# Decoder layer on one core: GpSimd's context columns ahead of two reciprocals, one context unit between the turns of the normalised rows, and the second probabilities parted before the third exponentials

## The reference, cut to what matters

```python
x = x + _L0_attn_ref(_layernorm(x), W_A, W_V, W_O, b_O)
x = x + _L0_xattn_ref(_layernorm(x), ctx_1024, ctx_1024, WK, WV, WQ)
x = x + _L0_ffn_ref(_layernorm(x), router_w, wg_r, wu_r, wd_r, wg_s, wu_s, wd_s)
```

## Time and profile before

| what | value |
|---|---|
| median of 3 runs | 569.32 us (568.86 to 569.55) |
| the profiled execution, its own time | 569.86 us |
| span of its instructions | 568.1 us |
| TensorE busy | 542.3 us, 95% of the span |
| VectorE, ScalarE, GpSimd busy | 424.9, 257.4 and 201.2 us |
| mean granted TensorE clock | 0.996 of full speed |

### The profile page before, as it was taken

How to read it: one execution, slowest core, us unless ns; L and a number is a source line. 1 busy time by engine, 2 the same in 40 slices (tenths; PEclk the granted TensorE clock), 3 DMA queues, 4 the chain that set the end, 5 groups by cost and what they waited for, 6 DMA issues and landing times. The chain is left out here.

```text
span 568.1 us, 12928 instructions
## 1 busy us (share of the span) xinstructions
PE 542.3 (95%) x4716; PEld 369.6 (65%) x4716; DVE 424.9 (75%) x1101; ACT 257.4 (45%) x521; POOL 201.2 (35%) x246
## 2 busy tenths in 40 slices
PE   5799889999999999999999999999999998999997
PEld 4576557566776668666776668666866685666455
DVE  5867878778776697778886888678876876777654
ACT  4566657435354445435353545435543334332332
POOL 4225752214522154314512343334421343133123
PEclk9999989999999999999999999999999999999999
DMA  7988696793459823693459643994189216200341
GB/s 241 305 282 304 198 388 201 165 348 117 113 123 269 281 67 84 139 303 121 112 121 270 204 111 78 213 304 111 48 175 324 69 60 132 58 1 1 91 98 38
DMA packets 90734, 94.70 MB, mean 167 GB/s; under 512 B 28224, under 2 KB 76224, under 8 KB 90432
## 3 DMA queue, kind: packets, MB, share of 16 engines
q1 hardware_dynamic: 90688, 94.09, 58.7%
HBM read 75.66 MB, written 12.12 MB: 155 GB/s over the span
## 5 line engine op out<-in xcount | busy, mean ns | idle before, releaser
L700 POOL TENSOR_TENSOR mid<-gated,mid 128x512 f16<-128x512 f32 x72 | 86.4, 1200 | 214.2 <-ACT mid L909 214.1
L909 ACT ACTIVATE mid<-gated 128x512 f16<-128x512 f32 x72 | 45.0, 625 | 83.4 <-DVEq L1268 80.1
L142 PE MATMUL wide<-w_d,mid 128*128 128x256 f16 x288 | 78.5, 273 | 0.0
L144 PE MATMUL wide<-w_d,mid 128*128 128x256 f16 x288 | 78.5, 273 | 0.0
L143 PE MATMUL wide<-w_d,mid 128*128 128x256 f16 x288 | 78.5, 272 | 0.0
L1246 DVE SCALAR_TENSOR_TENSOR gated<-gated,score 128x512 f32<-128x512 f32 x72 | 49.2, 683 | 37.7 <-ACT gated L904 37.4
L142 PE MATMUL rows<-h3T,w_gu 128*128 128x512 f16 x160 | 60.7, 379 | 0.3 <-DVEq L122 0.3
L142 PE MATMUL score<-h3T,w_gu 128*128 128x512 f16 x160 | 60.7, 379 | 0.2
L143 PE MATMUL rows<-h3T,w_gu 128*128 128x512 f16 x160 | 60.6, 379 | 0.0
L144 PE MATMUL rows<-h3T,w_gu 128*128 128x512 f16 x160 | 60.6, 379 | 0.0
L144 PE MATMUL score<-h3T,w_gu 128*128 128x512 f16 x160 | 60.6, 379 | 0.0
(11 more groups left out here) (251 smaller groups left out, 1423.5 us busy)
## 6 DMA issues: line engine op xcount, KB each, us to landing
toep<-z_scratch SPq DMA_DIRECT2D x14, 2048.0 KB, 18.0
stage<-comb_scratch SPq DMA_DIRECT2D x32, 512.0 KB, 8.4
toep<-z_scratch SPq DMA_DIRECT2D x4, 1024.0 KB, 10.3
x_bo<-in_x SPq DMA_DIRECT2D x8, 512.0 KB, 11.7
x_in<-in_xr SPq DMA_DIRECT2D x7, 512.0 KB, 11.1
qT<-q_scratch SPq DMA_DIRECT2D x7, 512.0 KB, 3.8
vx<-v_scratch SPq DMA_DIRECT2D x7, 512.0 KB, 5.1
out<-x_out SPq DMA_DIRECT2D x7, 512.0 KB, 3.3
```

Source lines behind the costliest of these rows:

```text
L142: pe.matmul(out, stationary[0], moving[0], start=start, stop=False, **kw)
L144: return pe.matmul(out, stationary[1], moving[0], start=False, stop=stop, **kw)
L700: pool.tensor_tensor(mid_slot(j, 1, late), gate_slot(j, late), mid_slot(j, 0, late), ALU.subtract).then_inc(mid_split.sem, 1)
L909: act.activation(mid_slot(j, 0, late), gate_slot(j, late), ACT.Copy).then_inc(mid_hi.sem, 1)
```

## The change

Five edits, all in iterations 0 and 1; no instruction is added or taken away.

1. GpSimd, iteration 0: the columns of context 1 stand ahead of the reciprocal deviation of sequence 1's first norm. ScalarE's part of these columns stands ahead of the units of context 0 rather than between them.
2. GpSimd, iteration 1: the columns of context 5 stand ahead of the last reciprocal deviation (second half of the third norm).
3. Iteration 1, ScalarE and VectorE: unit 2 of context 3 and the second probabilities (`part_prob(.., 1)`) stand ahead of the third exponentials (ScalarE) and their sums (VectorE); VectorE's statistics of the next rows stand later.
4. TensorE, iteration 1: unit 0 of context 5 stands between the two halves of the turn of `h3`.
5. ScalarE and VectorE: unit 0 of context 5 stands ahead of the parting of `h3T`, unit 1 behind it.

```diff
@@ gpsimd, second_iteration
                 reciprocal_deviation(it - 1, 2)
+                part_context_columns(5)
                 reciprocal_deviation(it - 1, 2, 1)
-                part_context_columns(5)
@@ gpsimd, iteration
                 for j in range(MID):
...
-                    if f and not m and j == 2:
+                    if f and not m and j == 0:
                         part_context_columns(1)
                     if n and j == (4 if d else 1):
                         reciprocal_deviation(it + 1, 0)
@@ scalar, second_iteration
                 part_prob(it, it - 1, 0)
-                exp_scores(it, it - 1, 2)
-                part_context_columns(4)
                 act.wait_ge(w_lo, GATES_2 + 1)
                 part_context(3, (2,))
                 part_prob(it, it - 1, 1)
+                exp_scores(it, it - 1, 2)
+                part_context_columns(4)
                 exp_scores(it, it - 1, 3)
...
                 normalise_x(it + 1)
+                part_context(5, (0,))
                 part_turned(it, it - 1, h3T, h3T_hi, "h3")
-                part_context(5, (0, 1))
+                part_context(5, (1,))
                 part_turned(it, it + 1, h1T, h1T_hi, "h1")
                 part_context(5, (2, 3))
@@ scalar, iteration
                 if f and not m:
-                    part_context(0, (0, 1))
                     part_context_columns(1)
-                    part_context(0, (2, 3))
+                    part_context(0, range(UNITS))
@@ vector, second_iteration
                 score_max(it, b, 2)
+                part_context(3, (2,))
+                part_prob(it, b, 1)
+                score_sum(it, b, 2)
+                score_max(it, b, 3)
+                attended(it, 0)
                 x_statistics(it + 1, range(2))
-                score_sum(it, b, 2)
-                part_context(3, (2,))
-                score_max(it, b, 3)
-                part_prob(it, b, 1)
-                attended(it, 0)
                 score_sum(it, b, 3)
...
+                part_context(5, (0,))
                 part_turned(it, b, h3T, h3T_hi, "h3")
-                part_context(5, (0, 1))
+                part_context(5, (1,))
                 part_turned(it, it + 1, h1T, h1T_hi, "h1")
@@ tensor, turn_halves
-            def turn_halves(it, use, src, made, b, second=None):
+            def turn_halves(it, use, src, made, b, second=None, between=None):
...
                 for c in range(C):
+                    if c == 2 and between is not None:
+                        context(between, (0,))
@@ tensor, second_iteration
-                turn_halves(it, "h3", h3, h_ready[2], b)
-                context(5, (0, 1))
+                turn_halves(it, "h3", h3, h_ready[2], b, between=5)
+                context(5, (1,))
```

## The result

The changed kernel takes 571.27 us (median of 18 runs, 570.18 to 573.04), the kernel before, run beside it, 569.66 us (18 runs, 568.86 to 570.56). The ratio is 1.0028, with a 95% interval of 1.0019 to 1.0036: slower by 1.6 us (1.1 to 2.1). The forecast was +1.15 us: 570.5 us from 569.32. On that base the ratio gives 570.9 us, near the upper end of the range of 569.3 to 571.0; the 571.27 stands against a kernel before that took 0.34 us more in this comparison than the 569.32. The profiled execution took 570.86 us, with a span of 569.1.

A forecast was written before the change was run, and what follows sets the result against it. TensorE, busy 542.3 of 568.1 us, was taken as the bound, so early shifts reach the end nearly whole. -0.75 + 0 + 0.70 + 1.2 = +1.15 us on 569.32 gave 570.5 us, range 569.3 to 571.0.

The forecast's parts named there:

- Edit 1, -0.75: Iteration 0: faster normalisations remove TensorE's 1.29 us gap, but the skewed load's landing caps the gain at 0.75 us.
- Edit 3, 0: Iteration 1, third probabilities: waits of 1.49 and 0.34 us become one of about 2.0, ending with GpSimd's columns; gain 0.
- Edits 2 and 4, the 2.27 us: Iteration 1, between the halves of `h3`'s turn: TensorE's 2.27 us gap and the low clock behind it go.
- the -3.85 of the rival: Rival, iteration 1: sequence 2's store lands by 77.4, so value units start at 80.5; -3.85 us, 565.5 us; chance 0.14.
- Edit 5, +0.70: Iteration 1: `h3T` queues behind the wait for sequence 2's store, so value units start at 84.3 instead of 83.61.
- The clock, +1.2: Behind TensorE's wait of over 4 us the clock falls, slowing `h1`'s turn and later work; +1.2 us, bounds 0 and 1.75.
- The old fall cost little.: Kernel before, behind the 2.27 us wait: the clock's fall cost little, since ScalarE waited for the store behind it.
- the clock did not stay up behind the long wait: Rival denied here: the mechanism holds, but the clock stays up behind the wait ahead of `h1`; -0.05 us, 569.3; chance 0.17.
- edit 1 did bring its gain: Rival denied here: in iteration 0 the skewed load or context 1's columns land too late, no gain; +1.9, 571.2; chance 0.10.

The follow-up runs named there:

- e2: Changed kernel, but ScalarE and VectorE part `h3T` ahead of unit 0 of context 5, as before the change; 569.47 us, ratio 0.9984 to the kernel before.
- e3: Changed kernel with context 5 written into buffers of its own, so its unit needn't wait for the store of sequence 2; 567.48 us, ratio 0.9951 to the kernel before.
- e4: Changed kernel with the store of sequence 2 issued ahead of iteration 1's 2 MB skewed loads; 566.73 us, ratio 0.9943 to the kernel before.
- e1: Kernel before with only the columns of context 1 moved ahead of the first reciprocal in iteration 0; 569.18 us, ratio 0.9987 to the kernel before.
- e7: Changed kernel with the iteration 0 move of context 1's columns taken back; 572.0 us, ratio 1.0041 to the kernel before.
- e6: Changed kernel plus sixteen matmuls, results never read, filling part of TensorE's wait ahead of the turn of `h1`; 570.74 us, ratio 1.0019 to the kernel before.
- e5: Kernel before with only the store of sequence 2 issued ahead of the skewed loads; 569.64 us, ratio 0.9997 to the kernel before.
- e8: Kernel before with only unit 2 of context 3 and the second probabilities moved ahead of the third exponentials; 569.83 us, ratio 1.0005 to the kernel before.
- e11: Same program as e9 (early store, second probabilities not moved), measured again; 565.97 us, ratio 0.9942 to the kernel before.
- e9: Changed kernel with the early store of sequence 2 and the move of the second probabilities taken back; 566.03 us, ratio 0.9938 to the kernel before.
- e10: e4 plus eight matmuls, results never read, ahead of unit 0 of context 4; 566.25 us, ratio 0.9936 to the kernel before.
- e12: Same program as e4 (changed kernel with the early store), measured again; 566.64 us, ratio 0.9942 to the kernel before.

## Why the prediction was right, step by step

The forecast was 570.5 us, +1.15 on the profiled execution; measured were +1.30 at the mark and +1.6 (1.1 to 2.1) by the ratio. The mechanism was the one forecast, and shown by undoing it in three ways (e2, e3, e4). Two sizes were off in opposite directions, edit 5 by -0.24 us and the clock by +0.38, so that the sum came nearer than its terms: that part is luck. With the measured terms it is -0.75 + 0 + 0.46 + 1.58 = +1.29.

- **Edit 1, -0.75.** Read at 38.29 against 39.04: as forecast, with the normalisation at 1.38 us (1.42) and the wait for the load where it was looked for. The ratios of e1 and e7 agree without being sharp. The wait for the load was only 0.24 us, where e2, whose trace has no early fall of the clock, had 0.68; the forecast had no such fall.
- **Edit 3, 0.** The wait was to be about 2.0 us and to end at 67.13 - 0.75; it was 2.06 and ended at 66.38. The 0 was right for this change. Its reason, the slack behind it, is right only while that slack exists: in e3, where it doesn't, the mark was 1.9 us worse than e4's, 1.7 of it a fall of the clock.
- **Edits 2 and 4, the 2.27 us.** They vanished, and the second half was done at 75.82 us (forecast 76.0 on the new clock). With a store in time they and edit 1 are worth the -3.85 of the rival within 0.3 at the mark (e4: -3.62); the 0.66 us that TensorE still waits for `h3T` was not in that sum.
- **Edit 5, +0.70.** The wait was forecast at 4.15 us and was 3.93; the value units came 0.12 us later than before, where -0.75 + 0.70 = -0.05 had been forecast. But the 0.12 has a part of the clock's fall in it: the turn took 1.62 us. With the clock up the value units start 1.00 us behind the turn (78.98 and 79.98 in e4's trace), which would be 83.32 here, 0.29 us earlier than before. So edit 5 by itself measured -0.29 + 0.75 = +0.46. The store wasn't faster (9.9 us, 10.0 before), and its issue came 1.0 us earlier, not 0.75. The advice to issue a DMA early and to wait late ("DMA: Bandwidth & Descriptors", section "Rules for kernel authors", of the Trainium skill) names both remedies: e2 waits later, e4 issues earlier, and the trace agrees with both.
- **The clock, +1.2.** This is the term that was mis-sized. It measured 1.58 us against the same stretch of e6 with the clock up, or 1.70 by the windows, both near the upper bound of 1.75. I had discounted it because a part of the low stretch might pass while TensorE waits. It did not: in windows of 0.5 and 1 us the clock is 1.00 up to 82.5, 0.71 from 82.5 to 83.0 and 0.50 from 83 to 86, so the whole fall lay on the work behind the wait. The page that I had set against it, "TensorE: Matmul & The Clock Gate", section "What's actually happening", of the Trainium skill, says that an idle array gets the half clock; that the fall was therefore certain was my reading of it. It came nearer than my discount, in the two profiles that have such a wait.
- **"The old fall cost little."** This was too low. e1 shows 1.02 us at the mark, of the 1.75 in the windows. The sum isn't touched, since it starts from the 83.61 that had the fall in it; but the marks here are compared with an execution of the kernel before that had paid for a fall of its own.

The rivals: the clock did not stay up behind the long wait in either profile that has it unfilled (the changed kernel, and e7 with 4.21 us), the store was not in time, and edit 1 did bring its gain.

## What to carry to other kernels

When an engine's instruction is moved ahead of another, look at what that instruction waits for, not at how long it takes: all that is queued behind it inherits the wait. Here two edits that are each worth nothing alone, an earlier store and the filling of a 2.27 us gap, together gave some 2.5 us of 570 (3.2 less the 0.7 of edit 1), and with the late store the order of two calls decided between loss and gain. And a long wait of TensorE can cost more than its length: here the wait of 3.93 us had 1.58 us of slower matmuls behind it. Price them in full, unless another wait already hides them.

## What the hardware showed that I had not expected

- **Waits near 2 us lower the clock in some executions and not in others.** Behind 1.95 us (near 10.7 us) the window of 10 to 15 us showed 1.00 in the kernel before, e2, e5, e8 and e11, and 0.66 to 0.73 in the changed kernel and in e1, e3, e4, e6, e7, e9, e10 and e12: e9 and e11 are the same program. Behind 2.06 to 2.08 us it fell in e2, e3 and e8 and stayed up in the changed kernel, e4, e6, e7 and e12. Behind 2.27 us it fell in the kernel before and e5 and stayed up in e1 and e8. The forecast took the single 1.95 us wait of the old trace as a sign that such a wait is harmless; one profile can't say that.
- **The lower level can be seen in single instructions.** At 0.77 the first matmul of 256 columns took 0.42 us instead of 0.27, and the eight turns of `h1` 1.62 instead of 1.16 (e4 and e6, which have the same order and a clock of 1.00 there).
- **The same store takes 4.0 or 9.9 us to land** by where it stands in the queue: 512 KB ahead of, or behind, the two 2 MB skewed loads. Those loads took 11.8 us when they were passed (e4), and 11.5 in the changed kernel and 11.8 in the kernel before, where they were not: no harm that shows.
